# Experts of a mixture layer on one Trainium2 core: each expert's weights are split four jobs sooner

## What is computed

```
logits = x @ router_w.T + router_b
topk_val, topk_idx = top_k(logits, 2);  weights = softmax(topk_val)
for each expert e:  h = x @ w1[e].T + b1[e]          # 128 -> 1024
                    h1, h2 = split(h);  y = (silu(h1) * h2) @ w2[e].T + b2[e]   # 512 -> 128
x = layernorm(x + sum over the two chosen experts of weight * y)
```

## Time and profile before

| | us |
|---|---|
| median of 3 runs | 2815.76 |
| the profiled execution | 2824.1 |
| its span in the profile | 2822.0 |
| TensorE (PE) busy | 2465.9 |
| VectorE (DVE) busy | 2043.2 |
| ScalarE (ACT) busy | 1442.9 |
| GpSimd (POOL) busy | 1183.1 |
| mean granted TensorE clock | 0.948 of full |

### The profile page before, as it was taken

One profiled execution on the slowest core, in us unless ns is written; L12 is line 12 of the kernel. 1 busy time (PEld: TensorE's weight loads), 2 busy tenths in 40 slices (PEclk: granted clock), 3 DMA queues, 4 the chain that ended last, 5 costly groups with the idle time before them and its releaser, 6 DMA issues.

```text
span 2822.0 us, 40142 instructions
## 1 busy us (share of the span) xinstructions
PE 2465.9 (87%) x14918; PEld 1133.0 (40%) x14918; DVE 2043.2 (72%) x3152; ACT 1442.9 (51%) x2509; POOL 1183.1 (42%) x748
## 2 busy tenths in 40 slices
PE   6679996698786987798679999999999999999897
PEld 4333332445233665466433333333333333333344
DVE  7676666633887994799468888788878888788542
ACT  5455553253654774477334555455544555455362
POOL 1135552120664551554204555455544555455530
PEclk9789997799998999899889999999999999999999
DMA  5000000101000000000010000000000000000000
GB/s 202 1 1 1 1 1 0 53 1 42 0 0 16 1 2 1 1 1 1 16 41 5 9 9 9 5 9 9 9 9 9 9 9 9 5 9 9 9 1 16
DMA packets 20831, 37.92 MB, mean 13 GB/s; under 512 B 10462, under 2 KB 12638, under 8 KB 19612
## 3 DMA queue, kind: packets, MB, share of 16 engines
q1 hardware_dynamic: 20636, 35.35, 3.6%
HBM read 32.99 MB, written 2.35 MB: 13 GB/s over the span
## 4 chain that ended last, share of the span: by engine, by line
PE 57%; DVE 29%; issue 7%; ACT 5%; POOL 1%; DMA 0%; ACTq 0%; DVEq 0%; SPq 0%; POOLq 0%
PE PS L2530 12%; PE PS L2521 12%; PE PS L1178 6%; DVE NR L2737 5%; PE PS L2491 5%; DVE W L2755 2%; DVE WK L815 2%; DVE NR L270 2%; DVE WK L2069 2%; PE PS L1160 2%; PE PS L1472 2%; DVE WK L2045 1%; DVE WK L267 1%; PE PS L2477 1%; PE PS L678 1%
## 5 line engine op out<-in xcount | busy, mean ns | idle before, releaser
L2737 DVE TENSOR_REDUCE NR<-PS 128x2 f32<-128x1024 f32 x512 | 626.1, 1223 | 210.8 <-PE PS L2492 210.7
L2632 ACT ACTIVATE WK<-PS 128x1024 f32<-128x1024 f32 x512 | 497.1, 1022 | 490.2 <-PE PS L2521 417.5
L2807 POOL TENSOR_TENSOR W<-W,WK 128x1024 f32<-128x1024 f32 x224 | 527.2, 2354 | 484.7 <-DVE W L2755 415.7
L2530 PE MATMUL PS<-WK,W 128*64 128x512 f32 x2048 | 494.1, 603 | 0.0
L2521 PE MATMUL PS<-WK 64*128 64x512 f16 (+1 forms) x4096 | 487.0, 378 | 0.0
L2755 DVE TENSOR_TENSOR W<-W,WK 128x1024 f32<-128x1024 f32 x224 | 284.6, 1271 | 14.4 <-ACT WK L2632 14.3
L2521 PEld LDWEIGHTS PS<-WK 64*128 64x128 f16 (+1 forms) x4096 | 199.7, 95 | 221.4 <-ACT WK L2632 6.5
L875 POOL TENSOR_TENSOR WK<-WK 128x512 f32<-128x512 f32 x128 | 165.6, 1294 | 180.3 <-ACT WK L768 180.3
L2491 PE MATMUL PS<-WK 64*128 64x512 f16 x512 | 196.5, 384 | 37.5 <-DVE NR L2737 35.3
L2530 PEld LDWEIGHTS PS<-WK,W 128*64 128x64 f32 x2048 | 124.1, 136 | 249.8 <-issue 172.7
L2492 PE MATMUL PS<-WK 64*128 64x512 f16 x512 | 196.5, 384 | 0.0
(11 more groups left out here) (364 smaller groups left out, 4367.8 us busy)
## 6 DMA issues: line engine op xcount, KB each, us to landing
XB<-l_rdens SPq DMA_DIRECT2D x62, 128.0 KB, 2.9
W<-in_mw SPq DMA_DIRECT2D x8, 512.0 KB, 12.5
W<-in_l2w SPq DMA_DIRECT2D x1, 3114.0 KB, 11.8
W<-in_f1w SPq DMA_DIRECT2D x1, 2816.0 KB, 18.9
W<-in_l3w SPq DMA_DIRECT2D x1, 2816.0 KB, 10.3
W<-in_f3w SPq DMA_DIRECT2D x1, 2816.0 KB, 9.7
W<-in_mw SPq DMA_DIRECT2D x8, 256.0 KB, 12.3
CBB<-in_cbb SPq DMA_DIRECT2D x1, 1360.0 KB, 8.3
```

Of the source, the lines that this page charges most:

```text
L2530: m = e.matmul(k.PS[64 * i:64 * i + 64, 4, :], self.V[:, kt, g, :], self.PTB[kt // 2 % 2][:, kt % 2, i, :], start=kt == 0, stop=kt == NT - 1)
L2632: e.activation(self.PTB[kt // 2 % 2][:, kt % 2, :, :], self.k.PS[:, 2 * (kt % 2):2 * (kt % 2) + 2, :], ACT.Exp, scale=1.0 / 64).then_inc(s ...
L2737: e.tensor_reduce(self.PM[ji % 2][:, u // 4, :, u % 4], self.k.PS[:, 6:8, :], AX.X, ALU.max).then_inc(self.maxes.sem)
L2807: e.tensor_tensor(ac, ac, p, ALU.add).then_inc(self.acc1.sem)
```

## The change

A constant `AHEAD = 4` is added. ScalarE splits eight parts (experts 0 and 1) ahead of the gates instead of four; in its loop the part done at i is number i + 8 instead of i + 4, as long as that is under 32, so its loop has 24 parts instead of 28. VectorE splits the four parts of expert 1 behind `gates` and ahead of its loop; in its loop the part done at i is number i + 7 instead of i + 3, from i = 1 to i = 24 instead of 28. Number n means expert n // 4, part n % 4. The number of instructions is the same, and all waits stay as they are.

```diff
+    AHEAD = 4
+
@@ act
-        for part in range(4):
-            w_high(0, part)
+        for n in range(4 + self.AHEAD):
+            w_high(n // 4, n % 4)
         e.wait_ge(*self.top(34))
@@ act, the loop
-            if i < 28:
-                w_high(i // 4 + 1, i % 4)
+            n = i + 4 + self.AHEAD
+            if n < 32:
+                w_high(n // 4, n % 4)
@@ dve
         self.gates(e)
+        for n in range(4, 4 + self.AHEAD):
+            w_low(n // 4, n % 4)
         for i in range(128 + 3):
@@ dve, the loop
-            if 1 <= i < 29:
-                w_low((i - 1) // 4 + 1, (i - 1) % 4)
+            n = i + 3 + self.AHEAD
+            if 1 <= i and n < 32:
+                w_low(n // 4, n % 4)
```

## The result

| | before | changed |
|---|---|---|
| median of 4 runs, us | 2815.67 | 2791.78 (2786.94 to 2794.84) |
| ratio to before, 95% interval | 1 | 0.9914 (0.9899 to 0.9929) |
| profiled execution / its span, us | 2824.1 / 2822.0 | 2786.9 / 2784.8 |
| L815 (now L820) of job 0 to job 31, us | 98.5 | 74.9 |

The change makes the kernel 24 us faster (20 to 28 by the interval); a median of 2793.7 was forecast. Lines have moved: first(i)'s first matmul L678 is now L680, L707 is L709, L721 L723, L745 L747, L749 L751, L768 L770, L774 L776, L798 L801, L809 L814, L815 L820, L875 L881.

What follows compares the result with a forecast made beforehand. TensorE's waits for VectorE's low part of the weights, 24.9 us in block 0, were taken as the bound. Job 31's hidden tile at 205.1 instead of 227.12 gains 22.1 us: 2815.8 - 22.1 = 2793.7 us, range 2785 to 2801.

Steps and rivals of the forecast that it cites:

- Ahead of the loop: Before block 0's loop: eight more splitting instructions each on ScalarE and VectorE fall in idle time and cost 0.
- The seven waits: TensorE's waits for the weights' low part at the first job of experts 1 to 7, 24.9 us, all go.
- the ring's own results: Results of the VectorE-ScalarE loop that sets the beat, 2.11 us per job in block 1; TensorE's next wait.
- More than a job to spare: In block 0, an expert's last weight part would be ready over a job before TensorE's first matmul needs it.
- The beat with a part: Block 0 jobs that carry a weight split take 2.445 us each; 22 jobs, 53.8 us.
- The other sum for it in the prediction: Block 0 beat by exclusive SBUF port use: 1.27 + 0.61 + 0.68 = 2.56 us per job, giving 2796.
- The gate copy: In block 0, the copy ahead of the SiLU delays it 0.47 us for six experts, charged 2.8 us.
- A: Rival: in block 0's loop the split pair is hidden and the beat is 2.16 us; 2785 us, chance 0.05.
- B: Rival: GpSimd and VectorE take turns badly in block 0, beat toward 3.15 us; 2806 us at the end, chance 0.05.
- C: Rival: block 0 ends earlier but a later stage waits that much longer; 2816 us, chance 0.04.
- D: Rival: TensorE's clock runs at half speed in block 0, 3.93 us per job; 2836 us, chance 0.04.
- The clock elsewhere: Behind block 0, half-speed clock stretches may shift somewhere; 2 us allowed.

Runs made afterwards that it cites:

- e8: Against the change, idle time ahead of the loop filled: ScalarE splits 18 parts before the gates' exponential, 6 parts left in the loop; 2785.96 us, ratio 0.9883.
- e5: The change with AHEAD = 28: all experts' weights split ahead of the loop, none in it; 2794.85 us, ratio 0.9916.
- e2: Only ScalarE's half of the change, VectorE's lines as in the kernel before; 2814.72 us, ratio 0.9999.
- e1: The change, with TensorE's first job of experts 1 to 7 again waiting for the hidden tile of the job just before; 2812.37 us, ratio 0.9988.
- e4: The change with AHEAD = 2: weights split two jobs sooner than before instead of four; 2796.12 us, ratio 0.9933.
- e6: e5 with a spare pair of one-SBUF-input instructions on VectorE in place of each of the 24 pairs; one run, 2801 us.
- e7: e5 with a spare pair of two-SBUF-input instructions on VectorE in the loop, results unused; one run, 2797 us.
- e9: e7 plus a spare pair on ScalarE where the high parts stood, results unused; one run, 2804 us.
- e10: The change with ScalarE's weight part moved ahead of the hidden tile's high part in its loop; 2788.79 us, ratio 0.9904.
- e11: e8 with ScalarE's weight part moved ahead of the hidden tile's high part in its loop; 2786.36 us, ratio 0.9898.
- e12: The changed kernel run once more as it is; 2790.37 us, ratio 0.9912.

## Why the prediction was right, point by point

- **Ahead of the loop, 0.** Held: the added instructions fell in idle time on both engines. e8 shows how much more it holds, and e5 where it ends: with 28 parts ahead instead of four, job 0 comes 12.8 us later.
- **The seven waits.** They went, and no other took their place: TensorE now waits for the ring's own results, 20.4 us at `down`, and keeps to its beat. e2 shows that VectorE's half was the cause, e1 that the wait itself holds two thirds of block 0's gain; 5.7 us of the other 7.7 I put down to the pair ahead of TensorE and the parts of the last jobs, and 2 stay open. "More than a job to spare" is e4: two jobs sooner were enough.
- **The beat with a part, 4.89 us for two jobs.** Measured 4.90 wherever no gate copy lies between. The other sum for it in the prediction, 2.56 us per job from three listed durations, was too long. My reading of the beat's cause was half of it: GpSimd against VectorE's two-input pair (e6, e7), and ScalarE's pair in front of the SiLU (e9, e10).
- **The gate copy, 0.47 us for each of six experts.** This is the term that was mis-sized. Four jobs took 10.0 us, not 2 x 4.89 + 0.47 = 10.25, so a copy cost 0.2 us. Block 1 has that already in the earlier trace rows: its four jobs take 8.64 us, 0.20 more than four steps of 2.11, so the copy is not slack there, and I charged the whole delay of the SiLU where only a part of it reached the beat. It isn't a fixed price either: in e10 the step with a copy is 2.73 us against 2.22, 0.5 us more. Job 2 to job 24 took 55.0 us (133.96 to 189.00) where 56.6 were forecast, jobs 24 to 31 took 14.95 for 14.97. The gain in block 0 was 23.6 instead of 22.1 us, by that term. With 0.2 us for a copy the forecast would have been 2792.1.
- **Rivals.** A, the hidden pair, would have been 66.6 us from 0 to 31 as in e5; the pair isn't hidden, although e8 and e11 come near by leaving only 6 in the loop. B did not come, save in one step of e12; halfway to its end would have been 2800 us, not the 2801 that the prediction took as the top of its range. C: the gain of the medians is as large as block 0's, so nothing behind it gave it back. D: the clock was 0.98 through block 0, though TensorE's weight load waited up to 1.2 us, 28 times, for VectorE.
- **The clock elsewhere.** I allowed 2 us. The four runs of the change spread over 7.9 us, so that was too little for a single run. The median of the change lies 1.9 us below the forecast, about 1.6 of it by the gate copy's term; that no more than 0.3 us is left is luck, for the runs differ by far more.

## What to carry to other kernels

Work that is done just in time must be finished before the consumer's lead is used up, counted in jobs along its own queue, not before the consumer's own position; here the last part was made two jobs behind the result that the consumer needed anyway, and two jobs sooner was enough. The sum of an engine's waits is not their price: 24.9 us cost nearly all of themselves, 14.3 us a quarter, 6.2 us nothing (block 0, less 0.35 us for each part that the loop had more). Then look where the moved work lands: ahead of a loop it is free up to the idle time of both engines, and within it its place in the stream, and the number of its SBUF inputs beside GpSimd, set its cost in this kernel.

## What the runs showed of the hardware that was not expected

- A VectorE pair of 0.6 us costs the ring between VectorE and ScalarE 0.00 us per job with one SBUF input and 0.19 us with two, beside the same GpSimd instruction (e6, e7).
- GpSimd can do two multiplications in a row, 2.54 us for both, while VectorE's 0.68 us instruction is stretched to 1.75 us: one step of one profile, 1.1 us longer than the others of its kind (e12). GpSimd's own instructions stretch too, from 1.27 to 1.52 us in block 0 after the change.
- With the same code ahead of it, the hidden tile of job 0 came between 128.7 (e1) and 130.6 us (e12) from the span's start.
